# Moving the next chunk's projection, transposes and gates into the output banks of a fused attention and mixture-of-experts layer

## The chip, the cores and the metric

The kernel runs on one core of one Trainium2 chip. The metric is the device time of one execution in microseconds (us). The kernel before took 1541.58 us (median of 3 runs, 1540.15 to 1547.16).

## The reference

Everything is float32. With `xn = layernorm(x)` for x of 4 x 1024 x 256, the result is `x + causal(xn) + ffn(xn)`:

```
causal: K, V = halves of xn @ W.T;  xn + softmax(xn K^T + causal mask) @ V
ffn:  q = xn Wq; k = (xn Wk_c) Wk; v = (xn Wv_c) Wv   (16 heads of 16, rotary on q and k)
      sa = softmax(q k^T / 4) @ v, all 1024 tokens, not causal;   sa = sa @ Wo
      x1 = rmsnorm(xn + sa) * norm1_w
      shared = swiglu(x1 @ W_shared_in) @ W_shared_out          (hidden 512)
      group = argmax of 2 gate logits; 2 best of its 4 experts; weights w = p_expert * p_group
      h = swiglu(x1 @ W1_shared);  routed = sum over the 2 experts of (h @ W2[e]) * w[e]
      ffn = rmsnorm(x1 + shared + routed) * norm2_w
```

## The kernel before

The program has five stages, each a block with one instruction stream for each engine, ordered by semaphores: projections, causal attention, head attention (the 16 steps of 4 heads of one batch), feed-forward part 1 and part 2. The change touches part 1 and the end of the head stage.

The 4096 tokens are cut into 8 chunks of 512 (`NCH`). Part 1 runs over the chunks. For each chunk c, TensorE does eight `hidden(c, f)`, f0 to f7 (line 1944): 12 matmuls of 512 columns each, three passes over high and low parts, into one of two two-bank PSUM buffers, `f_pair`. f0 to f3 make the routed hidden rows, f4 to f7 the shared ones. ScalarE takes one bank through Silu (L2031), VectorE multiplies by the other and frees the buffer (`gate_hidden`, L2094). For f4 to f7 ScalarE then rounds the product (L2024), and GpSimd makes its low part (`low_parts`, L1829). At the chunk's end `shared(c)` multiplies all this by the output weights (L1951, 48 matmuls) into four one-bank buffers, `f_ob`.

Between these parts the next chunk is made ready, at places set by constants. The program's names of the steps, which the text uses:

- OUT_AT (after f1): `WO`, the projection of chunk c+1 through Wo (L1120). VectorE adds `i_xn` to it (`residual`, L1201) and takes squares (L1209 to L1211); ScalarE takes the root; VectorE normalises (`normalise`, L1218) at NORM_AT, after f3, and there also weighs the experts of chunk c (`weigh`, small products, L1301 to L1306).
- TURN_AT (after f5): `XT`, the transposes of the normalised tokens (L1132), copied out by VectorE (`take_turned`, L1227) into `x1T`. At the same place VectorE does `head(c+2)` (L1195), attention values times inverse sums (`i_val` by `i_tot`).
- GATES_AT (after f7): `GATE`, the router's logits (L1142). VectorE's `route` reads them; ScalarE rounds x1T into `f_x1p` (L2020), VectorE makes its low part (L2079), and f0 of the next chunk waits for it.
- `classify` (VectorE, L1251 to L1280), between the sums of the shared outputs, sets each token's class flags and signals `flagged`. At RANK_AT (after f0) TensorE makes `RANK` (L1154, L1155), two matmuls of 60 columns that count tokens. VectorE's `place` (L1315 to L1324, 1.2 us from the first to the last) turns the counts into places, and GpSimd's `send` scatters the token numbers (four indirect DMAs, L1101).

The order in which `f_pair` is filled is a fixed list: f0, f1, WO, f2 to f5, XT, f6, f7, GATE. Two buffers take turns, so every fill waits until the last but one has been freed. In the last chunk WO, XT and GATE are absent, and VectorE has `locate` and `pick` (L1335 to L1362) after f1 and f2.

The transfers of part 1 are on SyncE's queue, in program order, each with its waits: `ya` (the causal result, L1881), `i_xn` (L934), the attention values (L917), the inverse sums. The softmax sums of a batch (two chunks) are loaded (L928), inverted by VectorE (`invert`, L1180), stored to the DRAM tensor rt_d (L931) and loaded back spread over partitions into `i_tot` (L923). Before, batch 0 goes this way in the head stage, batches 1 to 3 in part 1. GpSimd's `whole_ya(c+1)` (L1825, 128x1024) adds `i_xn` to `ya` after the last low part of chunk c.

## Time and profile before

| | |
|---|---|
| time, median of 3 runs | 1541.58 us |
| profiled execution, span from first to last instruction | 1551.4 us |
| TensorE busy | 1410.1 us, 91% |
| VectorE busy | 1148.2 us, 74% |
| ScalarE busy | 861.1 us, 56% |
| GpSimd busy | 357.3 us, 23% |
| part 1 on TensorE (first f0 to the last output) | 1053.70 to about 1364 us |
| mean granted TensorE clock | 0.942 of 2.4 GHz |

For the profiled execution only the span is given; nothing that lies around it has a number. The span is 9.8 us above the median of the timed runs. Busy times are shares of a whole program with five unlike stages; what a step of part 1 is worth must be read from part 1's own rows. `h_place`, `h_v` and `h_values` are buffers of the head stage whose space part 1 uses again, so rows of part 1 bear these names for x1, x1T, the routing's small tables and one of the two sets of rows. The DRAM side of a transfer is named by its tensor.

### The profile page before, as it was taken

Reading aid. Unit: us, or ns where it says so; the run is one execution under the profiler, and the core shown is the slowest. Engines: PE = TensorE matmul, PEld = TensorE weight load, DVE = VectorE, ACT = ScalarE, POOL = GpSimd, SP = SyncE. Lnnn points to the kernel's source line nnn. Section 1 sums busy time; section 2 is a strip of 40 time slices with the busy share of each in tenths; the row PEclk is TensorE's granted clock in tenths of the full one; section 3 lists DMA queues with packets and bytes.
Section 4 is the critical chain, followed back from the end, with each engine's and each line's share of the span. In section 5 each row is a group of like instructions: output and inputs, shape, how many; then the busy total and the mean of one; then the engine's idle time right before and its main releaser. Section 6 shows DMA issues by size and latency. Waiting matters only on the chain. (4 is left out here: it accounts for less than half of the span.)

```text
span 1551.4 us, 26402 instructions
## 1 busy us (share of the span) xinstructions
PE 1410.1 (91%) x9829; PEld 818.9 (53%) x9829; DVE 1148.2 (74%) x1786; ACT 861.1 (56%) x1573; POOL 357.3 (23%) x358
## 2 busy tenths in 40 slices
PE   7998799869999999999999999886899999979995
PEld 4665577623333333333333333335777777778884
DVE  3776756695999999999999999223566666646764
ACT  2454334205888888888888888662233333323332
POOL 0334902235050000000000001002233323345553
PEclk9999899855999999999999999868899999999998
DMA  6799776252443333333433331103455544255552
GB/s 194 272 323 338 261 214 143 49 99 62 70 117 60 56 54 54 51 49 63 63 63 63 63 64 49 51 7 87 132 148 147 156 134 121 92 181 174 172 171 64
DMA packets 115040, 183.47 MB, mean 118 GB/s; under 512 B 26389, under 2 KB 65705, under 8 KB 114917
## 3 DMA queue, kind: packets, MB, share of 16 engines
q1 hardware_dynamic: 90117, 124.55, 31.6%
q0 software_dynamic: 14336, 43.61, 9.8%
q10 hardware_dynamic: 10464, 13.64, 2.9%
q8 instruction: 81, 1.33, 0.4%
q14 instruction: 42, 0.34, 0.1%
HBM read 100.79 MB, written 81.88 MB: 118 GB/s over the span
## 5 line engine op out<-in xcount | busy, mean ns | idle before, releaser
L1679 DVE TENSOR_REDUCE i_saT<-h_sq 128x2 f32<-128x1024 f32 x512 | 621.8, 1223 | 44.4 <-PE h_sq L1556 32.8
L1645 ACT ACTIVATE h_p<-h_sk 128x512 f32<-128x512 f32 x999 | 543.4, 595 | 158.7 <-PE h_sk L1577 134.4
L1598 PE MATMUL h_po<-h_p,h_v 128*32 128x256 f32 (+1 forms) x3840 | 335.4, 422 | 6.7 <-ACT h_o L1652 4.9
L1577 PE MATMUL h_sk<-h_q,h_k 50*128 50x512 f32 x999 | 260.8, 511 | 16.4 <-ACT h_p L1645 15.8
L1556 PE MATMUL h_sq<-h_k,h_q 48*128 48x512 f32 x1024 | 224.9, 435 | 20.7 <-DVE i_saT L1679 16.8
L1577 PEld LDWEIGHTS h_sk<-h_q,h_k 50*128 50x128 f32 x999 | 97.7, 188 | 249.6 <-ACT h_p L1645 239.4
L1598 PEld LDWEIGHTS h_po<-h_p,h_v 128*32 128x32 f32 x3840 | 76.9, 110 | 184.9 <-issue 91.2
L1951 PE MATMUL f_ob<-w_experts,f_h 128*128 x1032 | 135.0, 286 | 14.3 <-issue 13.0
L1951 PEld LDWEIGHTS f_ob<-w_experts,f_h 128*128 128x128 f32 x1032 | 126.0, 189 | 24.0 <-issue 23.9
L1556 PEld LDWEIGHTS h_sq<-h_k,h_q 48*128 48x128 f32 x1024 | 104.1, 199 | 43.2 <-DVE i_saT L1679 38.9
L2031 ACT ACTIVATE h_v<-f_pair 128x512 f32<-128x512 f32 x64 | 38.1, 596 | 159.6 <-PE f_pair L1944 159.6
L1476 POOL COPY h_v<-h_values 128x512 f32<-128x512 f32 x14 | 8.6, 612 | 485.8 <-DMA h_values<-vh_d 485.8
L1944 PE MATMUL f_pair<-f_x1p,w_shared 128*128 128x512 f32 x384 | 95.9, 405 | 16.0 <-DVE h_place L1227 9.8
L1944 PE MATMUL f_pair<-w_routed,f_x1p 128*128 128x512 f32 x384 | 99.0, 414 | 6.2 <-DVE f_x1p L2079 6.2
L1944 PEld LDWEIGHTS f_pair<-f_x1p,w_shared 128*128 128x128 f32 x384 | 72.9, 192 | 36.3 <-DVE h_place L1227 10.3
L1944 PEld LDWEIGHTS f_pair<-w_routed,f_x1p 128*128 128x128 f32 x384 | 74.7, 198 | 23.8 <-DVE f_x1p L2079 7.9
L2094 DVE TENSOR_TENSOR h_place<-h_v,f_pair 128x512 f32<-128x512 f32 x48 | 32.9, 685 | 62.9 <-ACT h_v L2031 62.7
L1829 POOL TENSOR_TENSOR f_h<-h_place,f_h 128x512 fp32r<-128x512 f32 x32 | 43.1, 1347 | 142.1 <-ACT f_h L2024 142.1
L754 PE MATMUL a_out<-a_v,a_pT 128*128 128x256 f32 x432 | 65.6, 305 | 8.1 <-DVE a_v L835 8.1
L2107 DVE TENSOR_TENSOR f_h<-f_pair,f_h 128x512 fp32r<-128x512 f32 x43 | 29.7, 692 | 54.7 <-ACT f_h L2037 53.5
L727 PE MATMUL a_sc<-c_kT,c_qT 128*128 128x512 f32 (+3 forms) x192 | 67.8, 490 | 2.3 <-PEq L296 2.3
L754 PEld LDWEIGHTS a_out<-a_v,a_pT 128*128 128x128 f32 x432 | 57.2, 197 | 14.1 <-DVE a_v L835 8.5
(255 smaller groups left out, 1682.0 us busy)
## 6 DMA issues: line engine op xcount, KB each, us to landing
h_q<-q_d SPq DMA_DIRECT2D x84, 128.0 KB, 5.9
h_k<-k_d SPq DMA_DIRECT2D x84, 128.0 KB, 7.0
ot_d<-h_o ACTq DMA_DIRECT2D x32, 256.0 KB, 2.9
q_d<-t_parts SPq DMA_DIRECT2D x12, 512.0 KB, 5.0
k_d<-t_parts SPq DMA_DIRECT2D x12, 512.0 KB, 5.1
rows_d<-h_place SPq DMA_DIRECT2D x4, 1056.0 KB
rows_d<-f_rows SPq DMA_DIRECT2D x4, 1056.0 KB
p_xin<-in_L_attn_x SPq DMA_DIRECT2D x8, 512.0 KB, 5.1
```

The costliest lines, as they stand in the source:

```text
L727: ins = nc.tensor.matmul(sc[u % 2][:, c:c + w], qT[b % 2][:, k, i * P:(i + 1) * P], kT[b % 2][:, k, c:c + w], start=k == 0, stop=k == KD - 1)
L754: ins = nc.tensor.matmul(out[u % 2][:, 0:D], pT[u % 2][left][:, j, :], vp[b % 2][right][:, j, :], start=j == 0 and n == 0, stop=j == i and ...
L1556: ins = nc.tensor.matmul(sq[slot % 2][:, g, :], q6[r][at, p, i * P:(i + 1) * P], k6[r][at, p, half * CH:(half + 1) * CH], start=True, stop ...
L1577: ins = nc.tensor.matmul(spread_banks[bank_at(f + g)], k6[r][at, p, j * P:(j + 1) * P], q6[r][at, p, c * CH:(c + 1) * CH], start=True, sto ...
L1598: ins = nc.tensor.matmul(po[h * VW:(h + 1) * VW, at], vh[n % RING][:, j, h, :], probs[u % PR][:, h, at], start=j == 0 and part == 0, stop= ...
L1645: nc.scalar.activation(probs[u % PR][:, h, :], spread_banks[bank_at(f)], ACT.Exp, scale=DH ** -0.5).then_inc(exp_done, 1)
L1679: nc.vector.tensor_reduce(halfmax[n % 2][:, m, :], sq[slot % 2][:, :, :], AX.X, ALU.max)\
L1829: nc.gpsimd.tensor_tensor(h[LO][:, i, :], whole[i % 2], h[HI][:, i, :].bitcast(F32), ALU.subtract).then_inc(h_split, 1)
L1944: ins = nc.tensor.matmul(ps[:, half, :], left, right, start=n == 0, stop=n == len(terms) - 1)
L1951: ins = nc.tensor.matmul(to, lhs(left, i), weight(right, i), start=i == 0 and n == 0, stop=i == KH - 1 and n == len(terms) - 1)
L2031: nc.scalar.activation(sil[f % 2], fills.buffer(key)[:, 0, :], ACT.Silu).then_inc(sil_done[f % 2], 1)
L2094: nc.vector.tensor_tensor(to, sil[f % 2], fills.buffer(key)[:, 1, :], ALU.mult)\
```

## The change

Four edits.

1. WO, XT and GATE of the next chunk no longer take turns in `f_pair`; they go into the four `f_ob` banks. A new class `Banks` gives each fill its first bank and count, and one free-semaphore for each half (two banks). RANK and LISTS have bank 2, WO banks 0 and 1, XT banks 2 and 3, GATE bank 3, and OUT(c, j) bank j.
2. RANK_AT is 1 and not 0: the count matmuls and `place` come after f1.
3. On GpSimd `whole_ya(c+1)` comes right behind `send(c)`, ahead of the low parts of chunk c. On VectorE `take_turned` comes ahead of `head`.
4. Sums of batches 0 to 2 are loaded and inverted in the head stage. The inverses 1 and 2 are computed ahead of `head(1)` and stored at that stage's end, where SyncE waits for both stores. Part 1 has batch 3 alone. Its opening transfers have another order: values and inverse sums of chunk 2 go second, `ya` of chunk 1 behind `i_xn` of chunk 1.

```diff
+class Banks:
+    def __init__(self, whole, made, free, order):
...
+        for n, (key, first, count) in enumerate(order):
+            half = first // 2
+            theirs = range(first, first + count)
+            self.at[key], self.n[key] = (first, count), n
+            self.before[key] = max((latest[b] for b in theirs if b in latest), default=0)
+            users[half] += 1
+            self.turn[key] = users[half]
...
+    def store_inverses(self, eng, wait, b):
+        wait(self.inverted, b + 1)
+        self.chunk.store_inverses(eng, b, self.inverse[:, b, :], self.inverses_stored[b])
...
-                        chunk.load_sums(sp, 0, routing.inverse[:, 0, :], routing.sums_in[0])
+                        for b in range(B - 1):
+                            chunk.load_sums(sp, b, routing.inverse[:, b, :], routing.sums_in[b])
...
                 routing.load_inverses(sp, sp.wait_ge, 1)
+                for b in range(1, B - 1):
+                    routing.store_inverses(sp, sp.wait_ge, b)
+                for b in range(1, B - 1):
+                    sp.wait_ge(routing.inverses_stored[b], 16)
...
                 routing.place(dve, 0, first)
+                for b in range(1, B - 1):
+                    routing.invert(dve, b)
                 routing.head(dve, 1)
...
-        RANK_AT, OUT_AT, ROOT_AT, NORM_AT, TURN_AT, GATES_AT, LISTS_AT = 0, 1, 2, 3, 5, 7, 7
+        RANK_AT, OUT_AT, ROOT_AT, NORM_AT, TURN_AT, GATES_AT, LISTS_AT = 1, 1, 2, 3, 5, 7, 7
...
             for c in range(NCH):
                 if c:
-                    yield "RANK", c
...
+                    yield ("RANK", c), 2, 1
+                if c < LASTS:
+                    yield ("WO", c + 1), 0, 2
+                    yield ("XT", c + 1), 2, 2
+                    yield ("GATE", c + 1), 3, 1
+                else:
+                    yield ("LISTS", 0), 2, 1
                 for j in range(TPC):
-                    yield "OUT", c, j
+                    yield ("OUT", c, j), j, 1
...
                     routing.send(pool, c)
+                    if c < LASTS:
+                        whole_ya(c + 1)
                     for i in range(KH):
                         low_parts(c, i)
...
-                    if c < LASTS:
-                        whole_ya(c + 1)
...
                 load_ya(0)
+                load_values(2)
+                inputs.load_sums(sp, B - 1, routing.inverse[:, B - 1, :], routing.sums_in[B - 1])
+                load_xn(1)
                 load_ya(1)
-                for b in range(1, B):
-                    inputs.load_sums(sp, b, routing.inverse[:, b, :], routing.sums_in[b])
-                load_xn(1)
+                routing.store_inverses(sp, wait.ge, B - 1)
...
-                load_values(2)
...
-                        if f < B - 1 and c == 0:
-                            routing.invert(dve, f + 1)
+                        if f == 0 and c == 0:
+                            routing.invert(dve, B - 1)
...
                         if f == TURN_AT:
+                            if more:
+                                routing.take_turned(dve, c + 1, banks)
                             if c + 2 < NCH:
                                 routing.head(dve, c + 2)
-                            if more:
-                                routing.take_turned(dve, c + 1, fills)
```

TensorE at the start of chunk 1, before: f0, the two count matmuls, f1, the projection of chunk 2, f2 and f3.

```order
L1944 MATMUL f_pair<-w_routed,f_x1p 128x512 x12
L1154 MATMUL f_ob<-h_v 128x60
L1155 MATMUL f_ob<-h_v 128x60
L1944 MATMUL f_pair<-w_routed,f_x1p 128x512 x12
L1120 MATMUL f_pair<-w_out,i_saT 128x256 x8
L1944 MATMUL f_pair<-w_routed,f_x1p 128x512 x24
```

The same place in the changed kernel, up to the transposes and f6 and f7 (L1944 is now L1983, L1120 is L1154, and the count is L1188 and L1189).

```order
L1983 MATMUL f_pair<-w_routed,f_x1p 128x512 x24
L1188 MATMUL f_ob<-h_v 128x60
L1189 MATMUL f_ob<-h_v 128x60
L1154 MATMUL f_ob<-w_out,i_saT 128x256 x8
L1983 MATMUL f_pair<-w_routed,f_x1p 128x512 x24
L1983 MATMUL f_pair<-f_x1p,w_shared 128x512 x24
L1166 MATMUL f_ob<-h_v,h_place 128x128 x8
L1983 MATMUL f_pair<-f_x1p,w_shared 128x512 x24
```

The count has moved behind f1, and the projection and the transposes write to f_ob.

SyncE from the end of the head stage into part 1, before: store and loads of inverses 0, then the branches between stages, then part 1's opening transfers.

```order
L923 DMA i_tot<-rt_d 128x1x512 x2
L1457 UNCONDITIONAL_BRANCH
L1873 UNCONDITIONAL_BRANCH
L1881 DMA h_place<-ya_d 128x4x256
L1881 DMA f_rows<-ya_d 128x4x256
L928 DMA h_place<-ot_d 128x1x128 x3
L934 DMA i_xn<-xn_d 128x4x256
L1912 DMA rows_d<-r_zeros 104x10
L1913 DMA hidden_d<-r_zeros 128x4
L917 DMA i_val<-ot_d 64x1x512 x4
L931 DMA rt_d<-h_place 128x128
L923 DMA i_tot<-rt_d 128x1x512 x2
```

The same place in the changed kernel (L1881 is now L1920).

```order
L923 DMA i_tot<-rt_d 128x1x512 x2
L931 DMA rt_d<-h_place 128x128 x2
L1490 UNCONDITIONAL_BRANCH
L1912 UNCONDITIONAL_BRANCH
L1920 DMA h_place<-ya_d 128x4x256
L917 DMA i_val<-ot_d 64x1x512 x4
L923 DMA i_tot<-rt_d 128x1x512 x2
L928 DMA h_place<-ot_d 128x1x128
L934 DMA i_xn<-xn_d 128x4x256
L1920 DMA f_rows<-ya_d 128x4x256
L931 DMA rt_d<-h_place 128x128
```

Two stores of inverses now stand ahead of the branches that end the stage, and the values and inverse sums of chunk 2 stand ahead of everything but the first `ya`.

## Rows read from the trace of the kernel before

**Rows 1.** Stretch: us, busy PE, PEld, DVE, ACT, POOL; clock, DMA share, GB/s.

```profile
1142.00:1180.00 38.00, 35.73 (x195) 30.24 (x194) 25.98 (x70) 13.72 (x19) 11.81 (x9) 1.00 0.53 149
```

**Rows 2.** Waits of TensorE in part 1 up to 1345: total, times, longest.

```profile
PE f_ob L1154 <- DVE h_v L1280: 11.0, 7, 1.6
PE f_pair L1944 <- DVE h_place L1227: 9.8, 1, 9.8
...
PE f_pair L1944 <- DVE h_place L2094: 4.8, 7, 0.7
```

**Rows 3.** Timeline of TensorE, chunk 0: start, length, instruction, idle before and releaser.

```profile
1090.86 5.48 PE L1944 MATMUL f_pair<-f_x1p,w_shared 128*128 128x512 f32 x12 [9.82 <-DVE h_place L1227]
```

**Rows 4.** Timeline of VectorE and SyncE in the same stretch.

```profile
1088.37 1.29 DVE L1195 TENSOR_TENSOR i_saT<-i_val,i_tot 128x512 f32<-128x512 f32 x2 [10.46 <-DMA i_tot<-rt_d]
...
1062.90 0.63 SPq L931 DMA_DIRECT2D rt_d<-h_place  x1
1081.87 1.23 SPq L923 DMA_DIRECT2D i_tot<-rt_d  x2
```

**Rows 5.** Timeline of TensorE, chunk 2.

```profile
1142.63 2.92 PE L1944 MATMUL f_pair<-w_routed,f_x1p 128*128 128x512 f32 x12
1147.12 0.43 PE L1154 MATMUL f_ob<-h_v 128*128 128x60 f32 x2 [1.56 <-DVE h_v L1280]
...
1165.12 1.06 PE L1132 MATMUL f_pair<-h_v,f_rows 128*128 128x128 f32 x8
1166.89 5.86 PE L1944 MATMUL f_pair<-f_x1p,w_shared 128*128 128x512 f32 x24 [0.71 <-DVE h_place L2094]
...
1180.03 2.92 PE L1944 MATMUL f_pair<-w_routed,f_x1p 128*128 128x512 f32 x12
```

**Rows 6.** Timeline of VectorE, chunk 2.

```profile
1138.80 3.42 DVE L2079 TENSOR_TENSOR f_x1p<-h_place,f_x1p 128x1024 fp32r<-128x1024 f32 x1
...
1146.48 0.58 DVE L1280 TENSOR_TENSOR h_v<-h_v 128x12 f32<-128x12 f32 x3
...
1161.70 1.67 DVE L1218 SCALAR_TENSOR_TENSOR f_rows<-h_place,h_v,w_n 128x256 f32<-128x256 f32 x4
```

**Rows 7.** Timeline of TensorE: f1 behind two of the seven count waits.

```profile
1108.58 4.39 PE L1944 MATMUL f_pair<-w_routed,f_x1p 128*128 128x512 f32 x12
...
1259.83 4.59 PE L1944 MATMUL f_pair<-w_routed,f_x1p 128*128 128x512 f32 x12
```

**Rows 8.** The stretch 1110 to 1112, columns as in Rows 1.

```profile
1110.00:1112.00 2.00, 2.00 (x6) 1.52 (x6) 0.48 (x4) 0.00 (x0) 0.98 (x1) 0.50 1.01 391
```

**Rows 9.** Timeline of the head stage's end: ScalarE, VectorE, SyncE.

```profile
1048.18 0.33 ACTq L1656 DMA_DIRECT2D ot_d<-h_o  x1
1051.33 1.06 ACT L2020 ACTIVATE f_x1p<-h_place 128x1024 fp32r<-128x1024 f32 x1 [3.18 <-PEq L70]
...
978.24 0.93 DVE L1180 RECIPROCAL h_place<-h_place 128x128 f32<-128x128 f32 x1
1046.99 1.29 DVE L1195 TENSOR_TENSOR i_saT<-i_val,i_tot 128x512 f32<-128x512 f32 x2
...
981.18 0.57 SPq L931 DMA_DIRECT2D rt_d<-h_place  x1
983.98 1.31 SPq L923 DMA_DIRECT2D i_tot<-rt_d  x2
```

**Rows 10.** Timeline of GpSimd and SyncE, chunk 1 to 2.

```profile
1138.69 2.44 POOL L1825 TENSOR_TENSOR h_place<-h_place,i_xn 128x1024 f32<-128x1024 f32 x1
...
1165.72 1.27 POOL L1829 TENSOR_TENSOR f_h<-h_place,f_h 128x512 fp32r<-128x512 f32 x1 [11.18 <-ACT f_h L2024]
...
1152.34 0.36 SPq L1881 DMA_DIRECT2D f_rows<-ya_d  x1
```

**Rows 11.** Transfers issued 1150 to 1164: KB, us to landing.

```profile
f_rows<-ya_d SPq DMA_DIRECT2D x1, 512.0 KB, 10.1
```

**Rows 12.** Timeline of TensorE, last chunk.

```profile
1349.12 8.66 PE L1944 MATMUL f_pair<-f_x1p,w_shared 128*128 128x512 f32 x36 [1.35 <-DVE f_rows L2094]
```

More of the change, by code:

```diff
@@ L958, in released, with buffer, free_of, emptied @@
         return self.free_of(key), self.n[key] // len(self.buffers) + 1
+class Banks:
+    def __init__(self, whole, made, free, order):
+        self.whole, self.made, self.free = whole, made, free
+        self.at, self.n, self.before, self.turn = {}, {}, {}, {}
+        latest, users = {}, [0] * len(free)
+        for n, (key, first, count) in enumerate(order):
[5 more added lines that the diff above has]
+            self.turn[key] = users[half]
+            for b in theirs:
+                latest[b] = users[half]
+    def buffer(self, key):
+        first, count = self.at[key]
+        return self.whole[:, first:first + count, :]
+    def free_of(self, key):
+        return self.free[self.at[key][0] // 2]
+    def emptied(self, key):
+        return self.free_of(key), self.before[key]
+    def filled(self, key):
+        return self.made, self.n[key] + 1
+    def released(self, key):
+        return self.free_of(key), self.turn[key]
 class Room:
@@ L1791, in pairs_order @@
                     yield f, c
-                    if f == OUT_AT and c < LASTS:
-                        yield "WO", c + 1
-                    if f == TURN_AT and c < LASTS:
-                        yield "XT", c + 1
-                    if f == GATES_AT and c < LASTS:
-                        yield "GATE", c + 1
             for t in range(TILES):
@@ L1885, in load_xn @@
                     if c >= 2:
-                        wait.ge(*fills.released(("WO", c - 1)))
+                        wait.ge(*banks.released(("WO", c - 1)))
                     inputs.load_xn(sp, c, routing.xn_in)
@@ L2004, in _ @@
                         if f == GATES_AT and more:
-                            routing.gates(pe, c + 1, fills)
+                            routing.gates(pe, c + 1, banks)
                     shared(c)
@@ L2018, in high_parts @@
                     if c:
-                        act.wait_ge(*fills.released(("XT", c)))
+                        act.wait_ge(*banks.released(("XT", c)))
                     nc.scalar.activation(x1p[HI][:, :, :], x1T, ACT.Copy).then_inc(x1_rounded, 1)
@@ L2143, in _ @@
                         if f == OUT_AT and more:
-                            routing.residual(dve, c + 1, fills)
+                            routing.residual(dve, c + 1, banks)
                             routing.squares(dve, c + 1)
-                        if f < B - 1 and c == 0:
-                            routing.invert(dve, f + 1)
+                        if f == 0 and c == 0:
+                            routing.invert(dve, B - 1)
                         if f == 1 and not more:
@@ L2166, in _ @@
                     if more:
-                        routing.route(dve, c + 1, fills)
+                        routing.route(dve, c + 1, banks)
                         low_parts(c + 1)
```

23 lines of the change are left out of this document (9 added, 14 removed).

## The prediction, made before the changed kernel had run

> **What bounds the kernel now.** I read the busy times by stretch first. In a steady chunk TensorE is busy 35.73 us of 38 at full clock, VectorE 25.98 and ScalarE 13.72 [rows 1]. So in part 1 TensorE sets the pace, the other engines have slack, and only TensorE's own idle time can be won. The waits of TensorE in this stretch name that idle time [rows 2]: seven waits of the count matmuls for VectorE's flags, 11.0 us together; seven short ones for a freed PSUM buffer, 4.8 us; and a single one of 9.8 us. The timelines then tell what each hangs on, and which work fills the gap once it is gone.
>
> The long wait is in chunk 0 [rows 3, 4]. VectorE stands 10.46 us in `head(2)` for i_tot, until 1088.37; only behind it comes the copy of the transposes, which frees the f_pair buffer that f7 needs. The i_tot data is late since the store of the inverses was issued at 1062.90 and its load only at 1081.87, 18.97 us later. The same store and load in the head stage were 2.80 us apart (981.18 to 983.98) [rows 9]. After the wait f7 took 5.48 us, while 12 such matmuls take 2.92 in a steady chunk [rows 3, 5]: 2.56 us more are lost to a lower clock behind the pause.
>
> **The change, part by part.** I use chunk 2 as the model: from 1142.63 to 1180.03, 37.40 us [rows 5].
>
> *Count after f1.* The flags are set at 1146.48 + 0.58 = 1147.06 [rows 6]. f0 ends at 1145.55, f1 would end at about 1148.5 if nothing stood between. So the flags are 1.4 us early instead of 1.56 us late, and the wait goes. `place` now stands between the gates of f1 and the residual, where VectorE waits for the projection anyway; it costs nothing there. What is late next is nothing on this path. In the last chunk it is otherwise: VectorE does `locate` and `pick` there, and TensorE waits 1.35 us for the buffer of f3 [rows 12]. `place` (1.2 us) is now ahead of both, so VectorE's chain moves up by less than the count wait and that stall grows: I take 0.7 of the 1.57 us as won. Sum: 11.0 - 0.9 = 10.1 us.
>
> *Own banks for WO, XT, GATE.* f6 starts at 1166.89, 1.77 us behind the start of the transposes, of which 0.71 is the wait for the gate of f5 [rows 5]. With XT out of f_pair, f6 needs the buffer of f4, which is free by then. f7 needs that of f5, one part later. All 4.8 us go [rows 2]. The new waits of the banks: the projection needs OUT 0 and 1 of the chunk before, summed before the flags are set; OUT(c, 3) needs the logits read, which `route` does with its first instruction, while TensorE has three groups of nine matmuls of L1951 ahead of it. Cost 0.
>
> *The 9.8 us wait.* The inverses of chunk 2 are stored in the head stage, its values and sums are second on SyncE's queue in part 1, and the copy of the transposes stands ahead of `head`. Each of these alone would end the wait. Won: 9.82 + 2.56 = 12.4 us.
>
> *Half-clock episodes.* In two of the seven chunks f1 behind the count wait took 4.39 and 4.59 us, not about 2.9, and the granted clock there is 0.50 [rows 7, 8], the lower of the two levels. Both directly follow the count wait; the other five such waits have none. With the wait gone I take both as gone: about 1.6 us each, 3.2 us. Bounds: 0 and 3.2.
>
> *End of the head stage.* VectorE ends it with `head(1)` at 1046.99 [rows 9]. Now two reciprocals come first, 0.93 us each: the second ends at about 1048.9. Its store goes out then and lands 2.8 us later (981.18 to 983.98), 1051.7. Before, the last thing waited for was ScalarE's store, issued at 1048.18, and part 1 began at 1051.33. With the same way from a landed store to the first instruction (some 1.1 us, if ScalarE's store took 2 us; an estimate) part 1 begins at 1052.8. Loss: 1.5 us. Bounds 0.5 (the two waits overlap more) and 4 (the two stores in line, each 2.8).
>
> *`whole_ya` ahead of the low parts.* `ya` is issued at 1152.34 and takes 10.1 us [rows 10, 11]: 1162.44. The add of 2.44 us then ends at 1164.9. The low part of f4 began at 1165.72, now 1.56 earlier, 1164.16 [rows 10]. So it is 0.7 us late. The first that needs it is the gate of f6, some 4 us later, so 2 us of slack remain. I book 0 for it. On the other side, the add used to lie on VectorE's low part of x1T: that instruction took 3.42 us beside the add, which started 0.11 us earlier and lasted 2.44 [rows 6, 10]. The row reads as if VectorE stood still for the whole add. VectorE gains 2.2 us there, but TensorE does not wait for it. Where the add lands now it can hit `normalise`, which in the new schedule runs from 1160.14 to 1161.81 (rows 6, less 1.56), 0.6 us before the add. The transposes would start at 1163.56 (1165.12 - 1.56), so `normalise` has 1.75 us of slack, and a full block of 2.44 costs 0.7 us, with the gate of f4 behind it some more. Bounds 0 and 2.44 in each of seven chunks; nearest is the row that puts the landing behind `normalise`, so I take 0.2 us a chunk, 1.5 in all.
>
> The Trainium skill bears on this (SBUF — State Buffer, "Who interferes with whom"): a VectorE instruction with two SBUF inputs and a GpSimd instruction that reads SBUF shut each other out, whoever is first, for the whole instruction. The trace agrees in L2079. By that rule `normalise` and the small products of `weigh` are all exposed, and if `ya` landed 1 to 2 us earlier than before, every chunk would pay; this speaks against the edit, and is the second case below.
>
> **Sum.** 10.1 + 4.8 + 12.4 + 3.2 - 1.5 - 1.5 = 27.5 us. The profiled span of 1551.4 would become 1523.9. The span is 9.8 above the median of the runs; I take the same difference from the median: 1541.6 - 27.5 = 1514.1 us.
>
> **Rivals.**
>
> *A. The waits go, but something is given back in every chunk.* `whole_ya` blocks `normalise` or `weigh` (about 1 us a chunk, 7 us), or half-clock episodes stay or move elsewhere (3.2 us). For it: the add's new place is within 1 us of `normalise`. Against: both have slack. Gain 27.5 + 1.5 - 7 - 3.2 = 19: 1523 us.
>
> *B. Chunk 0 pays anew.* `i_xn` and `ya` of chunk 1 now stand behind 1 MB of values and sums and beside the scatters of GpSimd. The store of the inverses in this very stretch took up to 18.97 us [rows 4]. If `ya` of chunk 1 took as long, `whole_ya(1)` would hold up the low parts by some 5 us, and a late i_xn as much: gain 27.5 - 8 = 19.5, 1522 us. Against: before, the same load stood behind 0.7 MB and the residual did not wait for it.
>
> *C. Slower.* GpSimd now stands still for `ya` with the low parts behind it. From 2 us beyond the landing seen (12.1 us after issue) each further microsecond costs one in each of the six chunks 1 to 6. To eat the gain and 7.7 us more takes (27.5 + 7.7) / 6 = 5.9 us beyond, a landing 18 us after issue: 1549 us. The 18.97 us of rows 4 show that such a delay exists; against it stands that `ya` took 10.1 and nothing new shares its stretch.
>
> *D. No change.* The waits of TensorE are only put elsewhere, as VectorE's chain from the projection to the transposes turns out to be the limit: 1541 us. Against: VectorE is busy 26 of 38 us, and `normalise` ends 1.75 us before it is needed.
>
> **How the numbers follow.** Forecast 0.66, at 1509 to 1519. A 0.17, B 0.08, D 0.05, C 0.02; 0.02 for a gain above all of this. The best case is 10.1 + 4.8 + 12.4 + 3.2 - 0.5 = 30.0, 1511.6; with the noise of the runs (some 3 us) and a little for what I booked at 0, the low end is 1507. At the high end A with B's half, gain 15: 1527. Within 0.5% is what a measurement of this kernel can't tell from no change, 7.7 us. A and B are faster by more than that, so faster 0.93, same 0.05, slower 0.02.
>
> **What would show it.** Right: the list of TensorE's waits has no count wait but perhaps in the last chunk; f6 follows the transposes at once; a steady chunk takes 37.40 - 2.27 = 35.1 us; chunk 0 takes about 37 us from its f0 and not 49.9; the first instruction of part 1 comes 1.5 us later behind the head stage's last ScalarE store. L2079 takes about 1.2 us. For A: VectorE's L1218 or L1301 stretched to over 2 us beside L1825, and waits of TensorE for L1218 or L2094. For B: a wait of `whole_ya(1)` or of the residual for a DMA. For C: long waits of L1825 for `ya` and TensorE waiting for low parts in front of L1951. I am wrong if steady chunks stay above 36.5 us, or if the start of part 1 slips by more than 4 us.

## The result, and the profile after

The changed kernel took 1528.83 us (median of 13 runs, 1523.7 to 1539.34) against 1541.58 before: a ratio of 0.9919, 95% interval 0.9897 to 0.9941. By the ratio it is faster by 12.5 us, 0.8%, and not by the 27.5 that were forecast; 1528.8 lies 1.8 us above the upper end of the range.

The profiled span fell from 1551.4 to 1527.1 us. Not all of that is the change: part 1 begins at 1043.36 and not at 1053.70, in stages that the change hardly touches, and over all the kernels below this start lies anywhere between 1036 and 1056. So part 1 is compared by itself, from the first f0 to the last output: 310.6 us before, 297.7 after. That is 13.0 us, about the gain of the timed runs. These times and those of the experiments come from one profiled execution of each kernel. By chunk, from f0 to f0 (the last one to the last output), read from TensorE's timelines:

| kernel | chunk 0 | 1 | 2 | 3 | 4 | 5 | 6 | 7 | sum |
|---|---|---|---|---|---|---|---|---|---|
| before | 49.9 | 39.0 | 37.4 | 37.4 | 37.4 | 39.0 | 37.4 | 33.1 | 310.6 |
| after | 49.7 | 34.8 | 36.6 | 36.2 | 34.4 | 35.3 | 35.4 | 35.3 | 297.7 |

Three things stand out: chunk 0 won nothing, some chunks reach 34.4 and others not, and the last chunk lost 2.3 us (33.06 to 35.32).

The waits of TensorE in part 1 after the change (total, times, longest), which answer to [rows 2]:

```profile
PE f_pair L1983 <- DVE h_place L2133: 13.0, 4, 11.1
PE f_pair L1983 <- DVE f_x1p L2118: 6.4, 1, 6.4
PE f_pair L1983 <- DVE f_rows L2133: 2.2, 2, 1.4
PE f_ob L1196 <- DMA h_place<-idx_d,r_table: 2.1, 1, 2.1
PE f_ob L1990 <- POOL f_h L1868: 1.4, 3, 0.7
```

The seven count waits are gone and so is most of the short ones. But the 9.8 us wait of [rows 3] has a successor of 11.1 us, and waits for GpSimd's low parts (L1868) are new. The 6.4 us are the start of part 1, which stood at 6.2 before.

TensorE in chunk 2, answering to [rows 5]: the count, the transposes with f6 behind them, the output matmuls, the next f0.

```profile
1133.33 0.33 PE L1188 MATMUL f_ob<-h_v 128*128 128x60 f32 x2
...
1148.33 1.04 PE L1166 MATMUL f_ob<-h_v,f_rows 128*128 128x128 f32 x8
1149.12 5.84 PE L1983 MATMUL f_pair<-f_x1p,w_shared 128*128 128x512 f32 x24
...
1157.15 7.47 PE L1990 MATMUL f_ob<-w_shared_out,f_h 128*128 128x256 f32 x48 [0.50 <-POOL f_h L1868]
1164.46 0.86 PE L1983 MATMUL f_pair<-w_routed,f_x1p 128*128 128x512 f32 x3
```

The count starts without a wait, and f6 stands 0.79 us behind the start of the transposes and not 1.77. Those are edits 2 and 1 at work. The output matmuls wait 0.50 us for a low part and then take 7.47 us instead of 5.9.

**Chunk 0.** TensorE, where the first routed parts are done and f4 should begin:

```profile
1057.69 3.03 PE L1983 MATMUL f_pair<-w_routed,f_x1p 128*128 128x512 f32 x12 [0.16 <-DVE h_place L2133]
1071.85 7.46 PE L1983 MATMUL f_pair<-f_x1p,w_shared 128*128 128x512 f32 x24 [11.13 <-DVE h_place L2133]
```

VectorE, GpSimd and SyncE in the same stretch:

```profile
1056.14 0.95 DVE L1214 RECIPROCAL h_place<-h_place 128x128 f32<-128x128 f32 x1 [6.14 <-DMA h_place<-ot_d]
...
1067.27 1.22 DVE L1234 TENSOR_TENSOR h_place<-f_ob,i_xn 128x1024 f32<-128x1024 f32 x1 [9.63 <-DMA i_xn<-xn_d]
...
1073.35 2.38 POOL L1864 TENSOR_TENSOR f_rows<-f_rows,i_xn 128x1024 f32<-128x1024 f32 x1 [17.75 <-DMA f_rows<-ya_d]
...
1050.68 0.39 SPq L934 DMA_DIRECT2D i_xn<-xn_d  x1
```

Transfers issued from 1043 to 1053 (KB each, median us to landing), and below them the stretches 1050 to 1066 (columns as in Rows 1):

```profile
i_xn<-xn_d SPq DMA_DIRECT2D x1, 512.0 KB, 16.5
f_rows<-ya_d SPq DMA_DIRECT2D x1, 512.0 KB, 22.1
...
h_place<-ot_d SPq DMA_DIRECT2D x1, 64.0 KB, 11.0
```

```profile
1050.00:1058.00 8.00, 7.84 (x35) 6.34 (x34) 1.50 (x2) 1.02 (x2) 4.53 (x5) 1.00 0.89 175
1058.00:1066.00 8.00, 2.72 (x12) 1.88 (x10) 0.00 (x0) 1.46 (x2) 0.00 (x0) 0.95 0.10 11
```

The residual of chunk 1 stands 9.63 us for i_xn, with the gates of f2 and f3 behind it on VectorE, and TensorE behind those. i_xn took 16.5 us and `ya` of chunk 1 22.1, though from 1058 on the DMA engines are 10% busy. It is the place that rival B names, to which the prediction gave 0.08.

**The later chunks.** GpSimd and VectorE in chunk 2:

```profile
1148.59 2.40 POOL L1864 TENSOR_TENSOR f_rows<-f_rows,i_xn 128x1024 f32<-128x1024 f32 x1 [7.65 <-DMA f_rows<-ya_d]
1150.96 2.98 POOL L1868 TENSOR_TENSOR f_h<-h_place,f_h 128x512 fp32r<-128x512 f32 x2
...
1151.24 3.25 DVE L1228 TENSOR_TENSOR i_saT<-i_val,i_tot 128x512 f32<-128x512 f32 x2
```

`whole_ya` holds back two low parts, which then run back to back beside `head`; `head` takes 3.25 us where it took 1.29 in [rows 4], the gates and the last low parts come late, and TensorE's output matmuls wait. The stretch 1157 to 1160 shows what the short wait costs:

```profile
1157.00:1160.00 3.00, 2.85 (x14) 2.85 (x15) 1.98 (x6) 2.97 (x4) 1.38 (x2) 0.56 0.43 127
```

The granted clock is 0.56, near the lower level of 1.2 GHz, right behind the wait: 0.50 us of wait and some 1.6 of clock.

### The profile page after: what moved, and what is told of

The parts are those of the page before. It is cut to its first block and busy times, and to the rows that moved or that the text cites. A ratio compares the mean times of both kernels' runs of the same rounds, so it can differ in the third digit from the quotient of the medians.

```text
span 1527.1 us, 26396 instructions
## 1 busy us (share of the span) xinstructions
PE 1392.9 (91%) x9829; PEld 815.6 (53%) x9829; DVE 1142.1 (75%) x1786; ACT 859.6 (56%) x1573; POOL 357.4 (23%) x358
## 3 DMA queue, kind: packets, MB, share of 16 engines
q1 hardware_dynamic: 90117, 124.55, 33.1%
## 5 line engine op out<-in xcount | busy, mean ns | idle before, releaser
L1718 DVE TENSOR_REDUCE i_saT<-h_sq 128x2 f32<-128x1024 f32 x512 | 621.7, 1223 | 35.1 <-PE h_sq L1595 23.1
L1637 PE MATMUL h_po<-h_p,h_v 128*32 128x256 f32 (+1 forms) x3840 | 330.9, 417 | 6.8 <-ACT h_o L1691 4.9
L1616 PE MATMUL h_sk<-h_q,h_k 50*128 50x512 f32 x999 | 257.5, 504 | 16.6 <-ACT h_p L1684 15.9
L1990 PEld LDWEIGHTS f_ob<-w_experts,f_h 128*128 128x128 f32 x1032 | 125.5, 190 | 22.5 <-issue 22.5
L1595 PEld LDWEIGHTS h_sq<-h_k,h_q 48*128 48x128 f32 x1024 | 102.5, 196 | 43.2 <-DVE i_saT L1718 38.8
L1983 PE MATMUL f_pair<-f_x1p,w_shared 128*128 128x512 f32 x384 | 94.6, 402 | 15.1 <-DVE h_place L2133 12.9
L1983 PE MATMUL f_pair<-w_routed,f_x1p 128*128 128x512 f32 x384 | 94.7, 403 | 6.6 <-DVE f_x1p L2118 6.4
L1983 PEld LDWEIGHTS f_pair<-f_x1p,w_shared 128*128 128x128 f32 x384 | 72.5, 191 | 33.8 <-DVE h_place L2133 13.8
L1983 PEld LDWEIGHTS f_pair<-w_routed,f_x1p 128*128 128x128 f32 x384 | 73.1, 192 | 24.2 <-DVE f_x1p L2118 8.1
L2146 DVE TENSOR_TENSOR f_h<-f_pair,f_h 128x512 fp32r<-128x512 f32 x43 | 29.6, 691 | 49.4 <-ACT f_h L2076 49.4
L308 POOL TENSOR_TENSOR h_spare<-h_spare,t_sin 128x512 f32<-128x512 f32 x28 | 42.0, 1533 | 101.1 <-DVE h_spare L184 101.1
```

The source lines that it names most:

```text
L308: last = nc.gpsimd.tensor_tensor(swap[:, j, :], swap[:, j, :], sin[:, s, :], ALU.mult)
L1595: ins = nc.tensor.matmul(sq[slot % 2][:, g, :], q6[r][at, p, i * P:(i + 1) * P], k6[r][at, p, half * CH:(half + 1) * CH], start=True, stop ...
L1616: ins = nc.tensor.matmul(spread_banks[bank_at(f + g)], k6[r][at, p, j * P:(j + 1) * P], q6[r][at, p, c * CH:(c + 1) * CH], start=True, sto ...
L1637: ins = nc.tensor.matmul(po[h * VW:(h + 1) * VW, at], vh[n % RING][:, j, h, :], probs[u % PR][:, h, at], start=j == 0 and part == 0, stop= ...
L1718: nc.vector.tensor_reduce(halfmax[n % 2][:, m, :], sq[slot % 2][:, :, :], AX.X, ALU.max)\
L1983: ins = nc.tensor.matmul(ps[:, half, :], left, right, start=n == 0, stop=n == len(terms) - 1)
```

## Experiments

Part 1 means the sum of the eight chunks; ratios are to the kernel before, with their 95% intervals. An undisturbed chunk repeats to 0.01 us (34.41 in e4 and e5), but chunk 0 does not: kernels that differ there only by the zeros or the place of `whole_ya(1)` give 49.7, 51.9 and 51.2 (changed, e3, e4), and 42.7 and 45.9 (e1, e5). Less than some 3 us in chunk 0 is not read as an effect.

**e1: the old order of part 1's opening transfers, all else as changed**

```diff
                 load_ya(0)
-                load_values(2)
+                load_ya(1)
                 inputs.load_sums(sp, B - 1, ...)
                 load_xn(1)
-                load_ya(1)
-                routing.store_inverses(sp, wait.ge, B - 1)
...
+                load_values(2)
+                routing.store_inverses(sp, wait.ge, B - 1)
```

> The changed kernel with part 1's opening transfers in the order of before: ya of chunks 0 and 1, the sums of batch 3, i_xn of chunk 1, the two zero rows, and only then values and inverse sums of chunk 2 (the inverses are still stored in the head stage). Theory Q (queue): i_xn is late because 1 MB of values and sums stands ahead of it, and one queue serves in order. Then i_xn lands within 6 us of its issue, the 9.6 us wait of the residual and the 11.1 us wait of TensorE for f4 in chunk 0 go, and the time falls by about 11 us, unless head(2) waits a few us for its late values. Theory S (scatters): the four scatters of 4-byte elements of chunk 0 slow all transfers issued with them for some 20 us. Then the values of chunk 2 are late in place of i_xn and head(2) waits up to 5 us, i_xn still lands in time as before: gain 5 to 11 us. Theory Z (zero rows): the stores of 40 and 16 byte pieces do it: the same as S here. If i_xn is still over 10 us under way, Q is wrong.

1521.61 us, 0.9854 [0.977, 0.9937]; part 1 287.4, chunk 0 42.7. i_xn landed after 4.4 us and the wait for it is gone, but another took its place:

```profile
1077.54 1.29 DVE L1228 TENSOR_TENSOR i_saT<-i_val,i_tot 128x512 f32<-128x512 f32 x2 [6.34 <-DMA i_tot<-rt_d]
...
1081.49 7.52 PE L1990 MATMUL f_ob<-w_shared_out,f_h 128*128 128x256 f32 x48 [4.62 <-POOL f_h L1868]
```

Now i_tot is the transfer that comes late. The order chooses which consumer pays, and i_xn was the dearest: 7 us of chunk 0 come back (5 us in e5, which has chunk 0 at 45.9 against 51.2 in e4).

**e2: chunk 0's scatters behind its low parts**

```diff
-                    routing.send(pool, c)
+                    if c:
+                        routing.send(pool, c)
...
+                    if not c:
+                        routing.send(pool, c)
```

> The changed kernel with the four scatters of chunk 0 behind chunk 0's low parts instead of ahead of whole_ya(1). Theory S: without the scatters beside them i_xn and ya of chunk 1 land within 6 to 8 us (before 16.5 and 22.1), TensorE's wait in chunk 0 goes, about 11 us faster. Theory Q: no change for i_xn, 16 us, the same time within 2 us. Theory Z: no change either.

1531.83 us, 0.9935 [0.9893, 0.9976]; chunk 0 42.3, but chunk 1 47.8. With no scatter beside it i_xn still took 11.8 us behind the values. Once the scatters stood at 1080.5, i_xn of chunk 2, issued at 1078.87, took 23.3 us and the rows' store 23.7. The slow stretch moved with the scatters, and i_xn of chunk 2 was issued 1.7 us ahead of them: a transfer still under way is slowed as well as one issued behind.

**e3: the two rows of zeros in chunk 4**

```diff
-                zeros = routing.zeros
-                sp.dma_start(rows_d[N, :]...
-                sp.dma_start(hidden_d[N, :]...
...
+                    if c == 4:
+                        zeros = routing.zeros
+                        sp.dma_start(rows_d[N, :]...
+                        sp.dma_start(hidden_d[N, :]...
```

> The changed kernel with the stores of the two zero rows moved from part 1's opening to behind chunk 4. Theory Z: i_xn lands within 8 us and ya of chunk 1 too, about 11 us faster. Theories Q and S: i_xn still 16 us, the same time within 2 us; S allows that ya of chunk 1 lands a little sooner than 22 us.

1528.25 us, 0.9922 [0.9888, 0.9956]; chunk 0 51.9, i_xn 20.9 us. Moving the zeros away helps neither i_xn nor chunk 0.

**e4: `whole_ya` back behind the low parts**

```diff
                     routing.send(pool, c)
-                    if c < LASTS:
-                        whole_ya(c + 1)
                     for i in range(KH):
                         low_parts(c, i)
+                    if c < LASTS:
+                        whole_ya(c + 1)
```

> The changed kernel with whole_ya(c+1) back behind the low parts of chunk c, as before the change. Theory P (place of the add): GpSimd stands still for ya and then runs two low parts in a row, which shut VectorE's head out and delay f6's low part; with the add back, chunks 2, 3, 5 and 6 fall from 36.6, 36.2, 35.3 and 35.4 us to 34.4 to 34.8, about 5 us in all, and the count after f1 still has no wait. Its rival: the low part of x1T is stretched again to 3.4 us and the flags come late, so that the count wait returns (over 0.3 us a chunk) and nothing is won. Chunk 0 stays at about 49 us in both.

1523.1 us, 0.9901 [0.9861, 0.9941]; part 1 291.1, 6.5 less than changed. Chunks 1 to 6 all take 34.4 us, with no wait of TensorE in any; together they are 6.2 us below those of the changed kernel, and from e1 to e5, which differ by the same edit, 5.0. So edit 3's half on GpSimd costs 5 to 6 us. The timed runs agree in size (1523.1 against 1528.8), but their intervals overlap. Chunk 0 stayed at 51.2.

**e5: e1 and e4 together**

> The opening transfers in the order of before (e1) and whole_ya behind the low parts (e4) together. Measured so far in part 1: 297.7 us for the changed kernel, 287.4 with the order, 291.1 with the add back. If the two are independent: chunk 0 about 42.7 us with a wait of head(2) for i_tot (6 us), chunks 1 to 6 34.4 each, chunk 7 33.4: 282.5 us, some 15 us under the changed kernel, 1514 us in time. Rival: with the add back, i_xn of later chunks and head(2) meet other transfers and chunk 0 stays above 47 us.

1520.13 us, 0.9844 [0.9807, 0.988], the interval wholly below that of the changed kernel. Part 1 285.5, 3.0 above the sum expected, all of it in chunk 0 with 45.9; chunks 1 to 6 34.4. In chunk 0:

```profile
1087.74 1.29 DVE L1228 TENSOR_TENSOR i_saT<-i_val,i_tot 128x512 f32<-128x512 f32 x2 [9.29 <-DMA i_tot<-rt_d]
```

i_tot was issued by 1065.2 and came 22.5 us later.

**e6: e5 with chunk 0's scatters between its second and third low part**

```diff
+                        if i == 1 and c == 0:
+                            routing.send(pool, 0)
```

> e5, and the four scatters of chunk 0 behind its second low part instead of at its start. Theory Q and S together (a queue in order, and scatters that slow what is issued beside them): values and i_tot of chunk 2 come before the scatters, the 6.3 us wait of head(2) and the 4.6 us wait of TensorE for low parts in chunk 0 go, chunk 0 falls to about 37 us: 5 us under e5. What is issued beside the later scatters (ya or values of chunk 1 to 3) has slack. Rival Q alone: i_tot of chunk 2 still takes over 20 us and chunk 0 stays at 42 us.

1519.95 us, 0.9863 [0.9829, 0.9898]: the same as e5, where 5 us were expected. Chunk 0 fell to 40.9 and not to 37, chunk 1 rose to 40.1 (i_xn 15.4 us, the rows' store 17.1).

**e7: e4 with the count after f0 again (edit 2 undone, own banks kept)**

```diff
-        RANK_AT, ... = 1, ...
+        RANK_AT, ... = 0, ...
```

> The kernel of e4 (whole_ya behind the low parts) with the count matmuls and place after f0 again, as before the change. Flags are set at about 4.4 us into a chunk and f0 ends at 2.9: TensorE should wait 1.2 to 1.6 us in each of seven chunks, 35.7 to 36.0 us a chunk instead of 34.41; some 10 us slower than e4, less in the last chunk, where it saves a stall. Rival: the own banks alone made the count wait go, then chunks stay at 34.4.

1543.21 us, 1.0007 [0.9981, 1.0033]; part 1 310.8, 19.6 above e4. The count waits are back and longer than in [rows 2]:

```profile
PE f_ob L1188 <- DVE h_place L2140: 8.0, 4, 2.0
PE f_ob L1188 <- DVE f_rows L2140: 6.0, 3, 2.0
```

They name VectorE's sum of the outputs, which now frees the count's bank and stands behind `classify`: 14.0 us, the rest, as in [rows 7], slower matmuls behind them. Without edit 2, edit 1 loses what it brings.

**e8: e4 with edit 4 undone (batches 1 to 3 inverted in part 1 again)**

```diff
-                        for b in range(B - 1):
-                            chunk.load_sums(sp, b, ...)
+                        chunk.load_sums(sp, 0, ...)
...
+                    if c % 2 == 0:
+                        routing.store_inverses(sp, wait.ge, c // 2)
...
-                load_values(2)
-                inputs.load_sums(sp, B - 1, ...)
+                load_ya(1)
+                for b in range(1, B):
+                    inputs.load_sums(sp, b, ...)
...
+                load_values(2)
...
-                        if f == 0 and c == 0:
-                            routing.invert(dve, B - 1)
+                        if f < B - 1 and c == 0:
+                            routing.invert(dve, f + 1)
```

> The kernel of e4 with the fourth edit undone: sums of batches 1 to 3 loaded, inverted and stored in part 1, with the transfers of part 1 in the order of before. The copy of the transposes still stands ahead of head. If the moved inverses are what made chunk 0's i_xn late (through their order), i_xn lands within 6 us of its issue and the residual does not wait. Then head(2) waits for i_tot as before, until some 35 us into the chunk, but with the copy of the transposes ahead of it f7 is not held. Chunk 0: 44 to 48 us, between before (49.9) and e1 (42.7). Rival: the store of the inverses lands sooner than 18.9 us and chunk 0 is at 37 us; then the fourth edit was worth nothing.

1523.38 us, 0.9858 [0.9815, 0.9901]; part 1 288.8, only 3.3 above e5, which has the same order of the loads. Chunk 0 took 49.0:

```profile
1097.36 7.94 PE L1985 MATMUL f_ob<-w_shared_out,f_h 128*128 128x256 f32 x48 [10.29 <-POOL f_h L1861]
```

So the moved inverses are worth some 3 us at most of the 12.4 booked for chunk 0: the timed runs of e8 and e5 can't be told apart, and 3 us is what chunk 0 varies by. Edit 4 as it was made, with its new order, shows no gain: e4, which has all of it, stands at 291.1, 2.3 us above e8, which has none. The copy of the transposes ahead of `head` does not help by itself: the wait goes from f7 to the low parts of f6 and f7.

**e9 and e11: e5, and the changed kernel, without chunk 0's scatters**

Both leave the tokens of chunk 0 out of the lists, and the waits for these four scatters out of the program.

```diff
-                    routing.send(pool, c)
+                    if c:
+                        routing.send(pool, c)
...
```

> The order of transfers of e5 with chunk 0's four scatters left out (the tokens of chunk 0 are then missing from the lists; everything else is done). In e5 the inverse sums of chunk 2, issued at 1065.2, landed at 1087.7, 22.5 us later, and TensorE waited 7.6 us. Theory S (the scatters of chunk 0 slow every transfer beside them): i_tot lands within 8 us, head(2) follows the copy of the transposes at once and takes 1.3 us, TensorE has no wait of over 1 us in chunk 0 behind its first f0, and the chunk takes 37 to 39 us and not 45.85. Rival H (the 1 MB of hidden rows stored at 1072.5, or the values' own 64-partition pieces, do it): i_tot lands 15 us or more after its issue also now, and the wait stays at 5 us or more.

> The changed kernel with chunk 0's four scatters left out (the tokens of chunk 0 are missing from the lists), its order of transfers as it is. In the changed kernel i_xn took 16.5 us and ya(1) 22.1, and TensorE waited 11.1 us. Theory S alone: i_xn lands within 8 us, no wait in chunk 0, which takes 37 to 39 us and not 49.7. Theory Q+S (values and inverse sums ahead in the queue are slow by themselves, as the 11.8 us of i_xn with the scatters put later say): i_xn still takes 11 to 13 us, the residual waits 4 to 5 us, TensorE's wait for f4 is 5 to 7 us, and the chunk takes 42 to 45 us.

One run each: 1504.67 and 1518.62 us. In e9 chunk 0 took 36.4 us, part 1 279.0, and `head(2)` had no wait:

```profile
1061.31 2.13 DVE L1228 TENSOR_TENSOR i_saT<-i_val,i_tot 128x512 f32<-128x512 f32 x2
```

In e11 i_xn took 9.5 us, the sums 10.7, TensorE waited 2.22 us, and chunk 0 took 38.8 against 49.7. So of chunk 0's loss some 9 to 11 us hang on the four scatters (512 numbers of 4 bytes); e11 stays 2.4 us above e9, with the megabyte ahead of i_xn, which is no more than chunk 0 varies by. These are single runs, but the kernels that leave nothing out say the same of one transfer. The 64 KB store of the inverses behind that megabyte took 21.5, 22.8 and 22.0 us where the scatters stood beside it (e1, e10, e12), 8.9 without them (e9), 10.0 where it landed ahead of them (e6), and 8.1 and 8.2 where it went out behind their landing (e13, e15).

**e10: e5 with `head(2)` behind the sums of chunk 0**

```diff
-                            if c + 2 < NCH:
+                            if c and c + 2 < NCH:
                                 routing.head(dve, c + 2)
...
+                    if c == 0:
+                        routing.head(dve, 2)
```

> e5 with head(2) moved in VectorE's order from behind the copy of the transposes in chunk 0 to behind the sums of that chunk's shared outputs, all scatters in place. It is first needed by the projection behind f1 of chunk 1. If the late inverse sums cost time only because VectorE's gates and GpSimd's low parts stand behind head(2): the landing stays some 20 us after its issue, but the 7.6 us wait of TensorE is gone, chunk 0 takes 38 us and part 1 about 278 us against 285.5; the time is some 7.6 us under e5's, about 1513 us. Rival: the landing slips on or the projection of chunk 2 waits for head(2); then chunk 1 takes 37 us or more and under 5 us is won.

1527.93 us, 0.9877 [0.9803, 0.9952]. Chunk 0 took 36.2, where 38 was expected, but chunk 1 53.5:

```profile
1110.22 1.23 DVE L1234 TENSOR_TENSOR h_place<-f_ob,i_xn 128x1024 f32<-128x1024 f32 x1 [18.33 <-DMA i_xn<-xn_d]
```

```profile
i_xn<-xn_d SPq DMA_DIRECT2D x1, 512.0 KB, 16.8
idx_d<-h_v,r_sent_to POOLq DMA_INDIRECT x4, 11.6
```

SyncE's values of chunk 3 wait for `head(2)`, and i_xn stands behind them; both fell beside the scatters of chunk 1. I had not looked at that queue. By this run chunk 1's scatters do the same as chunk 0's once large transfers stand around them.

**e12: e10 with i_xn ahead of the values, and `head(2)` behind the low part of x1T**

```diff
-                    if c + 3 < NCH:
-                        load_values(c + 3)
                     if c + 2 < NCH:
                         load_xn(c + 2)
+                    if c + 3 < NCH:
+                        load_values(c + 3)
...
+                    if c == 0:
+                        routing.head(dve, 2)
```

> e10 with two orders changed so that no large transfer is issued beside the scatters of chunk 1: i_xn of a chunk stands ahead of the values on SyncE's queue, and head(2) stands behind the low part of x1T of chunk 1, ahead of the sums. In e10 i_xn of chunk 2 went out at 1093.3, behind the values that wait for head(2), with the scatters from 1092 on, took 16.8 us, and TensorE waited 16.1 us. Theory S2 (any scatter slows whatever large loads are issued just before or beside it, not only chunk 0's): i_xn is issued before 1085 and lands in under 8 us, the values of chunk 3 are issued 6 us or more ahead of the scatter, chunk 0 takes 36 to 38 us, chunk 1 34.4 to 36, part 1 about 279 us in all (no scatter in chunk 0: 279.0), and the time is 1508 to 1516 us, a ratio of 0.978 to 0.983. Rival F (the chunk with the second scatter is slow whatever goes out when): i_xn or the inverse sums of chunk 3 still take over 12 us and chunk 1 takes over 38 us.

1521.51 us, 0.9897 [0.985, 0.9944]; part 1 293.9 and not 279. Chunk 0 took 36.1 and i_xn was in time, but chunk 1 took 41.0:

```profile
1098.27 0.18 DVE L1249 RECIPROCAL h_v<-h_v 128x4 f32<-128x4 f32 x1 [5.06 <-DMA rows_d<-h_place]
```

This time it was the store of the rows, issued at 1081.99, landed 16 us later. The same store held VectorE up 3.4 and 3.1 us in chunks 2 and 3, which took 37.4 and 37.2.

**e13: e5 with the values of chunk 2 issued when chunk 0's scatters have landed**

```diff
+                sp.wait_ge(routing.sent[0], Routing.SENDS)
                 load_values(2)
```

> e5 with the values and inverse sums of chunk 2 (1 MB) issued only when the four scatters of chunk 0 have landed; i_xn and the zero rows stay beside the scatters. Theory V (the long landings need both, scatters and a megabyte or more queued beside them): the scatters land in 5 to 9 us as in the later chunks (6.4 to 9.5) and not 12 or more, the values go out some 17 to 20 us after the first f0, the inverse sums land within 8 us, head(2) waits 0 to 4 us and not 9.3, TensorE waits under 3 us and not 7.6 in chunk 0, which takes 37 to 40 us and not 45.85, and part 1 takes 278 to 281 us, the time 4 to 8 us below e5's. Rival W (the first scatters after the head stage are slow whatever is beside them): they land in 12 us or more, and since the values go out behind them head(2) waits longer than in e5, TensorE 8 us or more, chunk 0 takes 46 us or more.

1528.44 us, 0.9898 [0.9861, 0.9936]; chunk 0 49.5. The megabyte is not what makes the scatters late: the last one took 16.9 us with almost nothing beside it, and chunk 0 is no shorter because the values go out only at 1075. Transfers issued 1058 to 1075, then two stretches:

```profile
idx_d<-h_v,r_sent_to POOLq DMA_INDIRECT x1, 16.9
```

```profile
1062.00:1066.00 4.00, 4.00 (x19) 3.28 (x18) 1.94 (x3) 3.74 (x5) 0.00 (x0) 1.00 0.03 2
1066.00:1070.00 4.00, 4.00 (x19) 3.23 (x18) 3.05 (x7) 1.45 (x3) 0.00 (x0) 1.00 0.00 0
```

The packets of the scatters are not what takes this time either. Packets of GpSimd's queue from 1054 to 1062, and all packets from 1062 to 1075:

```profile
q0 software_dynamic: 128, 0.00, 1.2%
```

```profile
DMA packets 2, 0.02 MB, mean 2 GB/s; under 512 B 0, under 2 KB 0, under 8 KB 0
```

The two are loads of instructions. All 128 packets of the four scatters (the four of chunk 1 have 128 as well) are recorded by 1062, and yet three of the four landings came at 1068.0, 1072.1 and 1074.9.

**e14: e5 with four such scatters sent 100 us earlier**

```diff
+        for j in range(TPC):
+            pool.indirect_dma_start(self.warm_d, bass.IndirectOffsetOnAxis(self.sent_to[1][:, j:j + 1], 0),
+                                    self.tokens[:, j:j + 1], None).then_inc(self.warm, 16)
+        pool.wait_ge(self.warm, self.SENDS)
```

> e5 with four scatters of the same shape sent some 100 us earlier, at the end of GpSimd's constants in the head stage, into a tensor that nobody reads; all else as in e5. In the last run chunk 0's own scatters took 14.0 us (median) to land with hardly anything beside them, those of later chunks 6.4 to 9.5. Theory U (the first scatters of the program are slow because they are the first): the four early ones take 12 us or more and chunk 0's own then 6 to 10, the inverse sums of chunk 2 land within 10 us and not 22.5, TensorE waits under 2 us in chunk 0 and not 7.6, which takes 36 to 39 us and not 45.85, part 1 279 to 280 us and the time some 6 to 9 us below e5's. Rival P (the place in the program does it, its neighbours at the start of part 1): the early ones land in under 8 us, chunk 0's still take over 12, and chunk 0 stays at 44 us or more, the time within 3 us of e5's.

1518.5 us, 0.9842 [0.9789, 0.9895], as e5. i_tot was issued by 1051.1 and `head(2)` began at 1073.94, 22.8 us later; chunk 0 took 44.4. Being the first scatters of the program is not the cause. The early ones went into a tensor of their own, so being the first into `idx_d` is not ruled out.

**e15: e13 and e3 together**

> The last run but one (values and inverse sums of chunk 2 issued only when chunk 0's scatters have landed) with the two rows of zeros stored in chunk 4 and not beside these scatters. Theory Z2 (stores in pieces of 16 and 40 bytes and the scatters' own 4-byte pieces hold each other up): the scatters land in under 9 us and not 14 to 17, the values go out some 17 us after the first f0 and not 27, chunk 0 takes 37 to 41 us and not 49.5, part 1 279 to 283 us. Rival N (no neighbour in SyncE's queue is the cause): the last scatter lands 12 us or more after its issue, chunk 0 takes 44 us or more; then the cause stays open.

1524.71 us, 0.9855 [0.9782, 0.9929]; chunk 0 49.4. With i_xn alone beside them, and landed after 3.9 us, the scatters took

```profile
idx_d<-h_v,r_sent_to POOLq DMA_INDIRECT x4, 13.4
```

us in the median, three of them landing at 1071.5 to 1078.9, when nothing of SyncE's queue had been under way since 1062.1. None of its transfers but i_xn can bring it about.

## Why the prediction was wrong

- **The step that failed: "The 9.8 us wait. ... Each of these alone would end the wait. Won: 9.82 + 2.56 = 12.4 us."** Chunk 0 won 0.2 us. The old wait did end, and one of 11.1 us came from the transfers put in the old ones' place. I laid the late i_tot to the order of the store and its load; the runs show that what is under way beside chunk 0's scatters, or issued behind them, is slow. In the kernel before, the store at 1062.90 of [rows 4] is just such a transfer. The last of its scatters, and the landing of the store; below them the landing of a store of the same size in e9, without scatters and behind twice as many bytes of values and sums:

```profile
1063.07 0.96 POOL L1101 DMA_INDIRECT idx_d<-h_v,r_sent_to  x1 [0.31 <-issue]
rt_d<-h_place SPq DMA_DIRECT2D x1, 64.0 KB, 18.9
```

```profile
rt_d<-h_place SPq DMA_DIRECT2D x1, 64.0 KB, 8.9
```

  Without the scatters chunk 0 takes 36.4 us (e9), the "about 37" of the prediction. "Each alone" was wrong as well: e8 has the copy ahead of `head` and waits 10.3 us. Rival B named the place and the 18.97 us, but priced it at 8 us and not 12.2, and held against it that the residual "did not wait for it" before. What decides is that the residual stands ahead of the gates of f2 and f3 on VectorE.
- **Count after f1**: right in mechanism. All seven waits are gone. e7 puts edit 2 at 19.6 us on top of the banks, more than the 10.1 booked, since with own banks an early count would wait for the sums too.
- **Own banks**: right. f6 follows the transposes. An undisturbed chunk takes 34.4 us (e4, e5) and not 35.1. Of the 0.7 us between, 0.3 is at f6 (0.79 against 1.77 us, where I had taken off the wait of 0.71 alone); I have not traced the rest.
- **Half-clock episodes**: right for the two behind count waits, which went. Others came behind the new waits, in chunks 0 and 2, as in rival A.
- **`whole_ya` ahead of the low parts**: mis-sized, 1.5 booked and 6.2 measured in chunks 1 to 6 (e4 against the changed kernel; 5.0 from e1 to e5). I looked at `normalise`, with 1.75 us of slack, and booked the delayed low parts at 0. `ya` landed before the low parts were due, `normalise` was missed, and the two low parts released together fell on `head`, which the same edit had put there.
- **Chunks 1 to 6 together** won 15.0 us, close to the 15.9 that the terms give them (9.4 of the 10.1, 4.8 and 3.2, less 1.5). This is two errors that cancel: 21.2 without edit 3's half on GpSimd (e5), less 6.2.
- **The last chunk** lost 2.3 us where I had 0.7 won. The waits of 0.89 and 1.35 us came as worked out. Not foreseen: the lists are gathered when the last scatters have landed, and these now go out after f1.

```profile
1333.38 0.26 PE L1196 MATMUL f_ob<-h_v,h_place 44*128 44x44 f32 x1 [2.08 <-DMA h_place<-idx_d,r_table]
```

  It was 0.33 us before, it is 0.3 with the count after f0 (e7), and 1.4 to 3.4 in the other kernels. Behind it the 48 output matmuls took 7.46 us and not 5.92, with a granted clock of 0.64 from 1333.6 to 1338.
- **End of the head stage**: mis-sized, 1.5 booked, 0.2 measured. From ScalarE's store to its first instruction in part 1 (which answers to [rows 9]):

```profile
1037.65 0.33 ACTq L1695 DMA_DIRECT2D ot_d<-h_o  x1
1040.99 1.06 ACT L2059 ACTIVATE f_x1p<-h_place 128x1024 fp32r<-128x1024 f32 x1 [3.37 <-PEq L70]
```

  3.34 us, before 3.15. The inverses' stores were issued at 1037.43 and 1038.24, on either side of ScalarE's, and the second landed 0.2 us behind it, at 1039.88. I had given its landing 2.8 us, the distance from the store to the load in [rows 9]; it took 1.6.

Added up for part 1: 27.5 and the 1.5 of the head stage's end, which lies outside it, make 29.0; less 12.2 in chunk 0, 3.0 in chunk 7 and 0.9 in chunks 1 to 6 leaves 12.9, against 13.0 measured. The best kernels found, e5 and e14, stand at 0.984 of before; e9 marks what chunk 0 would still give: 9.4 us below e5 there, 6.5 in part 1, as its last chunk took 2.9 longer.

What stays open: why chunk 0's scatters take 12.7 to 15.5 us in the median, and those of the later chunks 5.3 to 9.7 where no megabyte stands beside them (e2 and e10 have 15.7 and 11.6 in chunk 1). It is not the values, not the zeros, not that they are the first of the program, and not only the moment: in e2 they went out 39 us and in e6 26 us after the first f0, and still took 12.8 and 12.7. The time passes between their last packet and their landing (e13). And how they slow other transfers is not shown, only that they do.

## What to carry to other kernels

A wait for a transfer is not explained by the order of its issues alone: ask what else was under way when it was slow, and whether the new order puts another transfer into the same stretch, and then price the consumer that has the most work queued behind it on its engine. When an instruction of a helper engine is moved ahead, follow the ones it delays to where they now run, not only the moved one. Two edits can each look free and depend on each other, as the banks and the place of the count do here.

## What the runs showed of the hardware

- Small scatters can be slow on nearly idle DMA engines. In e13 the engines were 3% and then 0% busy from 1062 to 1070 and the last scatter landed 16.9 us after its issue, some 13 us after the last packet recorded of its queue. i_xn, issued just ahead of such scatters with nothing queued ahead of it, was not slowed (3.9 to 4.7 us in e1, e5, e10, e13 and e15). With a megabyte ahead of it, it took 9.5 and 11.8 us without scatters (e11, e2) and 16.5 to 21.8 with them (changed, e3, e4); behind them i_tot took 22.5 us (e5) and the store of the inverses 21.5 to 22.8 (e1, e10, e12).
- A large transfer alone beside a later chunk's scatters is slowed less: `ya` took 11.5 us in chunk 1 and 8.7 in chunk 2 of e5, against 3.6 to 7.1 for the first `ya` of part 1. With more there, e10 and e12 show 16 us.
- A VectorE instruction with two inputs beside GpSimd's work stretched from 1.29 to 3.25 us (`head`), and to 2.13 beside a single low part (e9). By the Trainium skill (SBUF — State Buffer, "Who interferes with whom") the two engines shut each other out for whole instructions; the rows of chunk 2 nearly agree: two halves of `head` (0.65 us each alone) and two low parts (1.27 each) are 3.8 us in turn, and the stretch from 1150.96 to 1154.49 is 3.5.
- The granted clock fell to its lower level behind a wait of 0.50 us in chunk 2, at 1.6 us in price. In the last chunk 36 matmuls behind a wait of 1.35 us took 8.66 us, the same as in [rows 12], at full clock. In e12 24 matmuls behind a wait of 0.50 us (chunk 2, f6) took 5.86 us, against 5.84 undisturbed. The length of the wait alone does not tell.
